# Cross attention and a mixture of experts on one core: scores in strips of 32 features, k and v multiplied at the head of a step

## The reference

```python
x = x + attention(layernorm(x), ctx)       # 64 sequences of 64 tokens, 256 features, float32
x = x + experts(layernorm(x))              # 32 experts, the best 4 of each token, and a shared one
# attention, 16 heads of 16 features, 64 keys to a sequence:
q = rms_norm(xn @ w_q.T + b_q, g_q);  k = rms_norm(ctx @ w_k.T + b_k, g_k);  v = ctx @ w_v.T + b_v
p = softmax(q @ k.T / 4)                   # per head, over the 64 keys of the token's own sequence
out = (p @ v) @ w_o.T + b_o
# a text branch with a mask has no keys here (the context is shorter than its start), and adds nothing
```

## Time and profile before

| | us |
|---|---|
| runs: median of 3 (lowest, highest) | 849.14 (848.76, 853.83) |
| the profiled execution | 854.02 |
| its span | 852.3 |

### The profile page before, as it was taken

How to read it: one execution, slowest core, us unless ns; L and a number is a source line. 1 busy time by engine, 2 the same in 40 slices (tenths; PEclk the granted TensorE clock), 3 DMA queues, 4 the chain that set the end, 5 groups by cost and what they waited for, 6 DMA issues and landing times.

```text
span 852.3 us, 22206 instructions
## 1 busy us (share of the span) xinstructions
PE 773.8 (91%) x6030; PEld 641.5 (75%) x6031; DVE 586.4 (69%) x2018; ACT 470.2 (55%) x1410; POOL 490.2 (58%) x700
## 2 busy tenths in 40 slices
PE   3899999999999999729999999999999998998995
PEld 2566666666666666508899899989989998888884
DVE  2578888888888888554566566656656665586767
ACT  2678888888888888514444444444444443332231
POOL 0126566666666666576555555555555556565666
PEclk9999999999999999768999999999999999999998
DMA  6345655555555555659444444444443442677785
GB/s 194 102 126 175 218 177 177 173 172 172 178 179 181 185 182 175 199 171 300 124 130 129 131 123 130 129 122 130 129 130 119 129 142 75 229 236 226 238 252 177
DMA packets 101890, 142.02 MB, mean 167 GB/s; under 512 B 16171, under 2 KB 83043, under 8 KB 101219
## 3 DMA queue, kind: packets, MB, share of 16 engines
q1 hardware_dynamic: 87267, 100.66, 40.1%
q0 software_dynamic: 14592, 40.99, 13.6%
HBM read 86.73 MB, written 58.82 MB: 171 GB/s over the span
## 4 chain that ended last, share of the span: by engine, by line
PE 76%; DMA 8%; DVE 6%; issue 4%; POOL 3%; SPq 2%; ACT 1%; POOLq 0%; DVEq 0%; ACTq 0%
PE bank L1244 9%; PE bank L1252 8%; PE bank L472 6%; PE bank L1266 6%; PE bank L1268 6%; PE bank L1277 4%; PE bank L1259 4%; PE bank L529 4%; PE bank L419 4%; PE bank L436 4%; PE bank L505 4%; PE bank L547 3%; PE bank L458 3%; DMA got<-yt_d 3%; DVE acc L1446 2%
## 5 line engine op out<-in xcount | busy, mean ns | idle before, releaser
L1371 POOL DMA_INDIRECT yt_d<-yo,name_i x160 | 157.7, 986 | 29.5 <-issue 19.9
L771 POOL DMA_INDIRECT xs_d<-rgu,sloti x128 | 128.8, 1006 | 39.7 <-issue 32.5
L1416 DVE TENSOR_TENSOR h<-bank,gated 128x176 f32<-128x176 f32 x160 | 54.6, 341 | 87.6 <-ACT gated L1330 87.1
L1244 PE MATMUL bank<-down_w,rdt 128*128 x320 | 97.6, 387 | 18.4 <-issue 17.2
L1252 PEld LDWEIGHTS bank<-ht,rd_w 88*128 88x128 f32 x640 | 96.5, 191 | 8.4 <-issue 0.4
L1326 ACT ACTIVATE rdt<-bank 128x128 f32<-128x128 f32 x160 | 44.3, 277 | 103.2 <-PE bank L1252 103.0
L1330 ACT ACTIVATE gated<-bank 128x176 f32<-128x176 f32 x160 | 50.7, 317 | 86.9 <-PE bank L1268 86.3
L1252 PE MATMUL bank<-ht,rd_w 88*128 88x128 f32 x640 | 97.6, 274 | 0.0
L1369 POOL TENSOR_TENSOR fence<-ones 128x1 f32<-128x1 f32 x160 | 29.5, 184 | 111.7 <-DVE name_i L1406 111.3
L1405 DVE COPY yo<-bank 128x256 f32<-128x256 f32 x160 | 67.2, 420 | 24.6 <-PE bank L1244 24.5
L1411 DVE COPY ht<-bank 88x256 f32<-88x256 f32 x160 | 67.3, 421 | 20.8 <-PE bank L1259 11.4
(11 more groups left out here) (163 smaller groups left out, 1934.7 us busy)
## 6 DMA issues: line engine op xcount, KB each, us to landing
xg<-xs_d SPq DMA_DIRECT2D x160, 128.5 KB, 2.1
got<-yt_d SPq DMA_DIRECT2D x32, 512.0 KB, 4.6
raw<-in_raw SPq DMA_DIRECT2D x32, 496.0 KB
v<-v SPq DMA_DIRECT2D x128, 34.0 KB, 1.9
xs_d<-in_spare SPq DMA_DIRECT2D x4, 1028.0 KB, 6.1
xin<-in_x SPq DMA_DIRECT2D x32, 128.0 KB, 3.5
ctxt<-in_ctxt SPq DMA_DIRECT2D x32, 128.0 KB, 3.9
xres<-in_x SPq DMA_DIRECT2D x32, 128.0 KB
```

Of the source, the lines that this page charges most:

```text
L771: nc.gpsimd.indirect_dma_start(xs_d, bass.IndirectOffsetOnAxis(sloti[:, b, k:k + 1], 0), rgu[:, b, k, :], None)\
L1244: nc.tensor.matmul(y_ps[b], rdt[:, b, :], weight(down_w, DOWN), start=True, stop=True)\
L1371: nc.gpsimd.indirect_dma_start(yt_d, bass.IndirectOffsetOnAxis(name_i[:, b, :], 0), yo[:, b, :], None)\
```

## The change

- GROUPS, GH from 2, 4 to 4, 2: a strip has 32 features and 2 heads. Scores are 16 products of 32x64 weights with 128 columns each, in the first halves of four banks. ktm has two masked copies in place of four (the loop at line 668 runs over GH).
- k and v are two products of 256 columns into the second halves of banks 0 and 1; turned q and turned k go to the second halves of banks 2 and 3.
- kv_in runs right behind x_turn, ahead of down_product and qk_turn. x2_turn runs behind scores.
- kv_in waits for the subtraction of the scores two tiles back, qk_turn for the one before its own; scores wait for k and v of the next tile to be copied out.
- ACT copies v right behind xn1t; DVE adds the bias to k behind gate_weights, a step earlier by its own count.
- The wait for bo_done in step 3 moves behind qk_turn.

```diff
-GROUPS, GH = 2, 4
+GROUPS, GH = 4, 2
+STRIP = P // GROUPS
...
-            s_ps = bank03[:, 0:GROUPS, :]
-            kv_ps = bank03[:, 2, :]
-            qkt_ps = bank03[:, 3, :].rearrange("p (c t) -> p c t", c=2 * CH)
+            s_ps = bank03[:, 0:GROUPS, 0:DIM]
+            k_ps = bank03[:, 0, DIM:2 * DIM]
+            v_ps = bank03[:, 1, DIM:2 * DIM]
+            qt_ps = bank03[:, 2, DIM:2 * DIM].rearrange("p (c t) -> p c t", c=CH)
+            kt_ps = bank03[:, 3, DIM:2 * DIM].rearrange("p (c t) -> p c t", c=CH)
...
-                    if past(i, 1):
-                        pe.wait_ge(kb_done, i)
-                        pe.wait_ge(v_done, i)
+                    if past(i, 2):
+                        pe.wait_ge(ssub_done, i - 1)
                     pe.wait_ge(ld_ctx[b], landed(i, 2, b))
-                    for c in range(CH):
-                        m = nc.tensor.matmul(kv_ps, ctxt[:, b, c, :], wkv[:, c, :], start=(c == 0), stop=(c == CH - 1))
+                    for part, k in ((k_ps, 0), (v_ps, DIM)):
+                        for c in range(CH):
+                            m = nc.tensor.matmul(part, ctxt[:, b, c, :], wkv[:, c, k:k + DIM],
+                                                 start=(c == 0), stop=(c == CH - 1))
...
                     pe.wait_ge(ktm_done, i + 1)
-                    if past(i, 1):
-                        pe.wait_ge(ssub_done, i)
+                    if live(i + 1, TILES):
+                        pe.wait_ge(kb_done, i + 2)
+                        pe.wait_ge(v_done, i + 2)
...
-                                feats = slice(64 * g, 64 * (g + 1))
-                                m = nc.tensor.matmul(s_ps[SEQ * n:SEQ * (n + 1), g, c * 256:(c + 1) * 256],
+                                feats = slice(STRIP * g, STRIP * (g + 1))
+                                m = nc.tensor.matmul(s_ps[SEQ * n:SEQ * (n + 1), g, c * P:(c + 1) * P],
                                                      qt[feats, b, c, SEQ * n:SEQ * (n + 1)],
                                                      ktm[feats, b, 2 * c + n, :, :], start=True, stop=True)
...
                     x_turn(s, ph)
+                    kv_in(s, ph)
                     down_product(s, ph)
                     qk_turn(s, ph)
+                    if at_step(s, 3):
+                        pe.wait_ge(bo_done, 1)
+                        pe.wait_ge(halves_done, 2)
                     p_turn(s, ph, 0)
...
                     q_in(s, ph)
                     p_turn(s, ph, 1)
-                    kv_in(s, ph)
                     scores_ready(s, ph)
+                    scores(s, ph)
                     x2_turn(s, ph)
-                    scores(s, ph)
                     p_times_v(s, ph)
```

More of the change, by code:

```diff
@@ L432, in p_times_v @@
                     for blk in range(PAIRS):
-                        group, c, hp = blk // 4, blk // 2 % 2, blk % 2
-                        pair = PAIRS // CH * c + GH // 2 * group + hp
+                        group, c = blk // CH, blk % CH
+                        pair = PAIRS // CH * c + group
                         for n in range(2):
@@ L480, in qk_turn @@
                     pe.wait_ge(kn_done, i + 1)
+                    if past(i, 1):
+                        pe.wait_ge(ssub_done, i)
                     for c in range(CH):
-                        nc.tensor.transpose(qkt_ps[:, c, :], qb[:, b, c * P:(c + 1) * P], ident[:, :])
+                        nc.tensor.transpose(qt_ps[:, c, :], qb[:, b, c * P:(c + 1) * P], ident[:, :])
                     for c in range(CH):
-                        m = nc.tensor.transpose(qkt_ps[:, CH + c, :], kb[:, b, c * P:(c + 1) * P], ident[:, :])
+                        m = nc.tensor.transpose(kt_ps[:, c, :], kb[:, b, c * P:(c + 1) * P], ident[:, :])
                     m.then_inc(qkt_psum, 1)
@@ L652, in body @@
                         nc.scalar.activation(xn1t[:, b, :, :], xnt_ps, ACT.Copy).then_inc(xnt_done, 1)
+                        act.wait_ge(kv_psum, i + 1)
+                        if past(i, 2):
+                            act.wait_ge(v2_in[b], landed(i, 2, b, 64) - 64)
+                        nc.scalar.activation(
+                            v17[:, b, :, :, 0:HD],
+                            v_ps.rearrange("p (r g d) -> p r g d", r=2, g=PAIRS),
+                            ACT.Copy).then_inc(v_done, 1)
                     e = s - 1
@@ L659, in body @@
                         for c in range(CH):
-                            nc.scalar.activation(qt[:, b, c, :], qkt_ps[:, c, :], ACT.Copy,
+                            nc.scalar.activation(qt[:, b, c, :], qt_ps[:, c, :], ACT.Copy,
                                                  scale=gqk[:, c:c + 1])
@@ L664, in body @@
                     if live(i, TILES):
-                        kt = qkt_ps[:, CH:2 * CH, :].rearrange("p c (n k) -> p (c n) k", n=2)
+                        kt = kt_ps.rearrange("p c (n k) -> p (c n) k", n=2)
                         for g in range(GH):
@@ L690, in body @@
                                              accum_out=ssq[:, b, 1:2]).then_inc(ssq_done, 1)
[L691 to L696, removed]
                     i, b = s - 5, (ph - 5) % 2
@@ L860, in soft_max @@
                     dve.wait_ge(s_psum, i + 1)
[L861 to L863 removed]
+                    nc.vector.tensor_reduce(smax[:, b, :, :], s_ps.rearrange("p g (h k) -> p g h k", k=SEQ),
+                                            AX.X, ALU.max).then_inc(smax_done, 1)
                 def soft(s, ph):
@@ L868, in soft @@
                         return
-                    sv = s_ps.rearrange("p g (h k) -> p (g h) k", k=SEQ)
-                    mv = smax[:, b, :, :].rearrange("p g h -> p (g h)")
                     dve.wait_ge(smax_done, i + 1)
                     nc.vector.tensor_tensor(
-                        prob[:, b, :, :].rearrange("p q (r k) -> p (q r) k", r=2), sv,
-                        mv.unsqueeze(2).broadcast_to([P, HEADS, SEQ]), ALU.subtract).then_inc(ssub_done, 1)
+                        prob[:, b, :, :].rearrange("p (g c) (r k) -> p g (c r) k", c=CH, r=2),
+                        s_ps.rearrange("p g (h k) -> p g h k", k=SEQ),
+                        smax[:, b, :, :].unsqueeze(3).broadcast_to([P, GROUPS, CH * GH, SEQ]),
+                        ALU.subtract).then_inc(ssub_done, 1)
                 def q_bias(s, ph):
@@ L883, in k_bias @@
                 def k_bias(s, ph):
-                    i, b = s - 1, (ph - 1) % 2
+                    i, b = s, ph % 2
                     if not live(i, TILES):
                         return
-                    if at_step(s, 1):
+                    if at_step(s, 0):
                         dve.wait_ge(ld_next, 16 * len(loads_next))
                     dve.wait_ge(kv_psum, i + 1)
-                    nc.vector.tensor_tensor(kb[:, b, :], kv_ps[:, 0:DIM], bk[:, :], ALU.add).then_inc(kb_done, 1)
+                    nc.vector.tensor_tensor(kb[:, b, :], k_ps, bk[:, :], ALU.add).then_inc(kb_done, 1)
                 def o_norm(s, ph):
@@ L1034, in body @@
                     gate_weights(s, ph)
+                    k_bias(s, ph)
                     norm2(s, ph)
```

4 lines of the change are left out of this document (removed).

## The result

The changed kernel takes **856.97 us**, median of 6 runs (855.77 to 857.62). The kernel before, in 6 runs beside it, took 848.95 (847.74 to 853.83). The ratio of the two is **1.0083**, with a 95% interval of 1.0063 to 1.0103: slower by 8.0 us. The forecast had 875, 26.4 more than its base. The sign was right and the size was three times too large.

What follows compares the result with a forecast made beforehand. It took the 10.27 us step as held about equally by PE's sequence and a chain mostly through ACT. +1.78 - 0.55 - 0.26 = +0.97 a step, 26.4 in all, gave 875 us, range 858 to 886.

Steps and rivals of the forecast that it cites:

- The sum is 10.32, the step itself: First stage: start-to-start links from x_turn mostly through ACT to the next x_turn add to 10.32, so this chain holds the step.
- k and v into the chain, +1.78: Between x_turn and down_product: the product of k and v delays qk_turn and ACT's qt by 1.78 us a step.
- ktm, -0.55: ACT between the two probt: two masked copies fewer gain 0.55, not 0.71, since the second probt waits for p_turn's second half.
- v out, -0.26: ACT behind xn2t: v's copy moves behind xn1t, where ACT waits anyhow, taking 0.26 us off the chain.
- Scores 0.60, ahead of x2_turn, under cover: PE: scores take 0.60 us at eight places, other end 1.13, with 1.02 us of cover before x2_turn, which waits for down_w.
- Scores and x2_turn in either order, nothing: PE: moving scores ahead of x2_turn counts nothing on the chain, since x2_turn waits for down_w.
- One more switch, on PE alone: Array shape switches once more a step, costing 0.12 us on PE's own sequence and nothing on the chain.
- DVE: o_turn starts near 9.0 us behind x_turn, ACT comes to ot only at 9.79, so nothing is added beyond the chain.
- The ramp, -0.7 for it and the last drain step: Output-bias wait no longer stops x_turn in the ramp and one drain step keeps ktm's gain: -0.7 us together.
- The two long steps, 71 to 94 us: Two steps holding 1.85 us of other waits absorb part of the delay, so they add 0.9 us together.
- the shorter chain: Rival: probt wait falls away and kv_in costs 1.72, +0.75 a step, or +0.4; 860 to 870 us; chance 0.15.
- PE sets the step: Rival: chain links have slack and PE's own sequence counts, step 9.97, 0.30 less, 840 us; chance 0.07.

Runs made afterwards that it cites:

- experiment 6: Kernel before with the change's order alone (k and v behind x_turn, v copied early), old strips, four ktm, x2_turn ahead of scores: 915.9 us, ratio 1.0807.
- experiment 3: Kernel before with two added ACT copies of 128x256 behind xn2t in each step: 852.61 us, ratio 1.0044, step 10.42.
- experiment 7: Changed kernel with x2_turn ahead of the scores again: 868.63 us, ratio to before 1.0245; its table splits the step at x2_turn for four kernels.
- experiment 8: Changed kernel with kv_in behind p_turn's first half, v behind ktm, k's bias behind norm2, x2_turn ahead of scores: 860.85 us, ratio to before 1.0125.

## Why the prediction was right in sign and wrong in size

**The step that failed** is the first of the forecast: "The sum is 10.32, the step itself ... So the step is held twice, by PE's own sequence and by this chain, about equally", and with it "putting work into the chain costs its full length". Start-to-start distances around any loop of the program sum to the period, whether it is tight or not. The check proved nothing. The chain is tight from x_turn to x2_turn, and there work did cost its full length (experiment 6). Behind x2_turn PE's order set the pace, with the scores in it, and ACT's way had 0.47 of slack (experiment 3), as waits too short to be listed. From the earlier trace rows, xn2t to egate is 1.74 before, of which v is 0.26; without it 1.48. After, the same link is 1.23. The rows of before that lie in it, ACT:

```profile
211.89 0.38 ACT L678 ACTIVATE xn2t<-bank 128x256 f32<-128x256 f32 x1 [0.68 <-PE bank L520]
212.35 0.42 ACT L685 ACTIVATE squares<-qb 128x256 f32<-128x256 f32 x1
212.67 0.19 ACT L685 ACTIVATION_READ_ACCUMULATOR squares<-qb 128x1 f32 x1
212.95 0.42 ACT L689 ACTIVATE squares<-kb 128x256 f32<-128x256 f32 x1
```

and DVE beside them, the biases of q and of k:

```profile
211.81 0.42 DVE L881 TENSOR_TENSOR qb<-bank,bq 128x256 f32<-128x256 f32 x1
...
212.42 0.41 DVE L890 TENSOR_TENSOR kb<-bank,bk 128x256 f32<-128x256 f32 x1
```

xn2t ends at 212.27 and the squares of q start at 212.35, 0.12 behind the end of DVE's qb (212.23). In the changed kernel they start at 214.56, 0.10 before xn2t's end (214.66). So ACT's next instruction can start 0.10 ahead of the end of the last, and 0.08 behind it is a wait of 0.18, which no view lists. The squares of k wait for kb (ends 212.83) in the same way. The other links that shrank are egate to ot (1.70 to 1.63), ot to project (0.45 to 0.41), project to x_turn (1.06 to 0.97) and down_w to xn2t (1.11 to 1.05). The waits before had shown part of it, and I hadn't used it:

```profile
ACT ot L715 <- PE bank L538: 1.2, 8, 0.2
```

A link that waits for something which isn't a link of the chain is slack.

**The sum again, with what was measured.** The after's links add to 10.66: 0.22 + 1.73 + 0.43 + 0.64 + 0.51 + 1.35 + 0.49 + 1.05 + 1.23 + 1.63 + 0.41 + 0.97. In the before's order (0.25 in place of 0.22 + 1.73, 1.90 in place of 1.35, v's 0.26 added) they are 9.77, within 0.03 of the 9.80 that the two copies gave. The change adds 0.89 to the chain (forecast 0.97), and 10.27 - 9.77 = 0.50 of it closes slack. That the rest comes out at the measured 0.38 is no further evidence, since both sums are distances from start to start and must differ by just that. The evidence is the 9.80, which another edit gave, and the halves of the step in the table of experiment 7. Ahead of x2_turn the forecast had +1.78 - 0.55 = +1.23, and +1.08 was measured. Behind it, the forecast had -0.26 for v, and -0.71 was measured. Of the 0.59 by which the forecast was too high, 0.45 is this second half: the scores, 1.03 of PE's 5.43 there, moved away, and the forecast had put that at nothing on the chain. So the path that sets the changed kernel was foreseen rightly, with nearly the right increments. What failed is the claim that it had set the whole step before.

Point by point:

- **k and v into the chain, +1.78.** Measured 1.73 (208.08 to 209.81), and 1.75 for the order alone. Right.
- **ktm, -0.55.** The second probt waits for the second half of p_turn, 1.35 from probt to probt, forecast 1.35. Right, and not 0.71.
- **v out, -0.26.** Right: it lies in the idle time behind xn1t.
- **Scores 0.60, ahead of x2_turn, under cover.** Measured 0.62, and in the changed kernel they start at 212.77, x2_turn at 213.75. The cover held. The Trainium skill (TensorEngine Tiling, Tiling Modes) lists eight tiles for an array split in 32x64. The 0.62 agrees with eight at once: four at a time would need 32 passes x 0.11 / 4 = 0.88.
- **Scores and x2_turn in either order, nothing.** Wrong, by experiment 7: 0.39 a step hang on it. This didn't change the forecast, since the change has the good order.
- **One more switch, on PE alone.** x2_turn to scores is 0.34 in experiment 7, as in the earlier trace rows. PE has room for it now.
- **DVE.** o_turn is at 216.50, 8.64 behind x_turn, forecast near 9.0; ot at 9.28, forecast 9.79. Nothing beyond the chain, right.
- **The ramp, -0.7 for it and the last drain step.** Measured -3.4 by the x_turn of step 4. Two waits of PE before,

```profile
19.34 0.41 PE L449 MATMUL bank<-ident,xn 128*128 128x128 f32 x2 [1.25 <-ACT up_w L726]
...
28.91 0.44 PE L449 MATMUL bank<-ident,xn 128*128 128x128 f32 x2 [2.22 <-DVE bo L1017]
```

  come to 0.80 and 1.31 after, both for DVE's xn, and what is left of the wait for the output bias is 0.34:

```profile
30.16 0.66 PE L422 MATMUL bank<-ident,prob 128*128 128x128 f32 x4 [0.34 <-DVE bo L1024]
```

  No experiment takes the ramp's parts asunder. That kv_in fits beside the wait for the first raw weights is my reading of the rows, not shown.
- **The two long steps, 71 to 94 us.** They held 1.85 beyond two steps. After, the same two take 21.35 in place of 22.39, like the others, so they get shorter by 1.0, where the forecast had 0.9 more; the step behind them takes 11.01.
- **Number of steps.** 28 x 0.38 = 10.6, less some 1.4 to the long steps, is the 9.2 seen.

The rival nearest to the truth was the shorter chain, where "some tenths more close up in ACT: +0.4", with 860 to 870. Its step is the one measured. Its time lacked the ramp's 3.4: 860 less that is 857, but the long steps weren't in it either, so that the sum meets 857 is in part luck. It had a chance of 0.15 and deserved more. "PE sets the step" was right of the kernel before behind x2_turn only and wrong of the one after, and the condition that I gave it (over 1 us to spare) was for a win; half of that existed.

## What to carry to other kernels

A loop of start-to-start distances that sums to the period is no evidence that it sets the period; for each link ask whether its start is given by the link before it, to the tenth, and count as slack whatever it waits for from elsewhere. An added copy that costs nothing shows slack in the stretch where it stands. An engine at 100% in the windows can still wait a tenth in every step: compare the distance between a release and the start behind it with a place where the wait is listed, and split the step at such a point. When work goes into a chain, its cost is its length less the slack there, and what is queued behind the delayed instruction (here the scores behind x2_turn) can be longer than the chain foreseen.

## What the runs showed of the hardware

- Two f32 copies of 128 x 256 on ACT in sequence cost 0.31 us each from start to start, with records 0.41 long (experiment 3), so there a gap of 0.0 between two records is a wait of about 0.1.
- Scores over 32 rows at eight places took 0.62 us for 32 passes of 128 columns; over 64 rows at four places 1.03 for 16 passes of 256.
- Splitting a product of 512 columns in two of 256 cost nothing to see: 1.73 us for eight passes in the changed kernel, 1.71 to 1.79 for four in nearly all steps of experiment 6.
- x2_turn started 0.14 to 0.15 us behind the end of the ACT copy that it waits for, in every step of the kernel before, of the changed kernel and of experiment 6; the second half of p_turn 0.05 behind the end of probt.
- At a granted clock of 0.55, p_times_v and rgu_in took 3.65 us, at 1.00 2.13 (experiment 6).
- On POOL a scatter of one choice took 0.96 to 1.15 us, with 0.18 to 0.30 of issue ahead of it, so three of them put an rstd behind them off by 3.7 us (212.19 to 215.89 in experiment 8).
